# Last context chunk of each batch loaded on its own, into 80 partitions instead of 128

## The chip, the cores and the metric

The kernel runs on one core of one Trainium2 chip. The metric is the device time of the whole program in microseconds (us), the median over several runs. A profiled execution has a time of its own and a span, from the first to the last instruction, in which the trace shows every engine.

## What is computed

The reference is one layer of a perceiver-like network in float32, on x (32 batches x 64 rows x 512) and a context (32 batches x 1601 rows x 512). Three blocks follow each other: attention of x over the context, self-attention of x, and a mixture of eight experts with a shared expert. The change touches only the first block, for each batch:

```python
Sim = (enc @ w1)[:, :, None] + (ctx @ w2)[:, None, :] + einsum('bid,bjd->bij', enc * w3, ctx) + b_sim
A = softmax(Sim, axis=2)                 # 64 x 1601
hq_hat = einsum('bij,bjd->bid', A, ctx)  # 64 x 512
feats = concatenate([enc, hq_hat, enc * hq_hat, enc * hc_bar], -1)
hcq = feats @ W_qv + b_qv                # 2048 -> 512
```

`enc` is x after a layer norm, `ctx` the context. The context is thus used twice: once transposed (the scores) and once with its rows on the partitions (the weighted sum).

## The kernel before

**Tiles.** Two batches make one tile t of 128 rows (64 + 64), so there are T = 16 tiles. For each tile the context of both batches (h = 0, 1) is read from HBM twice: `ctxT[h]`, four pieces k of 128 partitions x 1601, and `ctxN[h]`, 128 partitions x 13 chunks x 512. A chunk c holds 128 context rows; 12 chunks are full (JM = 12) and the thirteenth has the last JT = 65 rows. In HBM the thirteenth chunk is padded to 128 rows, and each partition's 13 chunks lie side by side, so a partition's share of neighbouring chunks is one contiguous run.

**Loads.** All of this is issued by SyncE (SP). `load_ctx_T` (L437) loads a tile's `ctxT` in 8 transfers. `load_ctx_N` (L448) loads `ctxN` in four parts q (NP - 1 = 4), each once for either h: parts 0 to 2 have three chunks, the fourth has chunks 9 to 12. There is one buffer of each, so every load first waits for TensorE to have used that part of the tile before: `sim_done` counts the k of the scores, `pv_done` the groups of the weighted sum. Each transfer adds 16 to `ctxN_in[q]`, so TensorE waits for 32 per tile. The first tile is loaded at the start of the program, `ctxN` of it right after one piece of `ctxT`; then come rows of x and the weight `w_qv` (L459 to L461), then the loads for tile 1. Tiles 6 to 15 are loaded in a hardware loop of SP.

**TensorE.** The first tile's scores have a way of their own, so as not to wait for its `ctxT`: `first_T(q)` (L1896) transposes part q of `ctxN` by 36 instructions on TensorE in four parts, `first_T_end` (L1906) the last 65 rows, and `first_similar` (L1880) makes scores of them. From then on a tile goes through `stage_a`: transposes of small tiles (L1860, L1838), `features` (L1930 to L1947), `spread_max` (L1964), `exp_T` (L1970, 13 transposes of the softmax's numerators), `attend` (L1992, the weighted sum over 13 chunks, with `combined_chunk` L1955 between groups of three) and `similarities` (L1880, the next tile's scores). Tiles 2 to 13 are in a hardware loop with two tiles to a round. In `attend` TensorE waits for `ctxN_in[c // 3]` at c = 0, 3, 6, 9. The last chunk is read as `ctxN[h][0:65, 12, :]` only.

**After the first block** come weights for the other two blocks, loaded when `sim_done` has reached its last count, and then self-attention, router and experts. They use no context.

Of the kernel before, what the change touches and what calls it, by code (L numbers as in the profile page):

```python
# [29 lines left out]
JM = J // P  # L30
JT = J - JM * P
JC = JM + 1
JB = [(c * D, min(D, J - c * D)) for c in range(-(-J // D))]
NP = 5
H, HD = 16, 32
# [27 lines left out]
def perceiver_layer(nc, x, ctx_n, ctx_t, w1, w23, b_sim, w_qv, b_qv, wq, wk, wv, wm, b_qk, bv, bm,  # L63
# [8 lines left out]
    with ExitStack() as stack:  # L72
# [3 lines left out]
        def sem(name):  # L76
            return stack.enter_context(nc.semaphore(name))
# [42 lines left out]
        def within(name, lo, *dims, dt=F32):  # L120

            with nc.sbuf_tensor(name + "_lead", [P, lo], F32):
                with nc.sbuf_tensor(name, [P, *dims], dt) as v:
                    return v
# [5 lines left out]
        with nc.sbuf_tensor("raw_ws1", [P, KD, FS], F32) as raw_ws1:  # L130
# [3 lines left out]
        stage_at = [(ZERO_AT - 5 * KD * D, ZERO_AT - 4 * KD * D), (ZERO_AT - 3 * KD * D, ZERO_AT - 2 * KD * D),  # L134
                    (ZERO_AT - KD * D, ZERO_AT + D)]
        stage_raw = [within(f"stage_raw{i}", lo, KD, D) for i, (lo, _) in enumerate(stage_at)]
        zero = within("zero", ZERO_AT, D)
        wr_sb = within("wr_sb", stage_at[-1][1] + KD * D + D, KD, P)
# [4 lines left out]
        split_ws2 = within("split_ws2", WS, 2, KF, D, dt=F32R)  # L143
        W_QV = 2 * KD * J + 2 * JC * D
        HQ = W_QV + 6 * KD * D + J + -(W_QV + J) % 16 + JC * P + 2 * D
        w_mid = within("w_mid", W_QV + KD * D, 2 * KD, D)
# [8 lines left out]
        def carve(*dims):  # L155
            n = 1
            for d in dims:
                n *= d
            v = arena[:, used[0]:used[0] + n]
            used[0] += n  # L160
            if len(dims) == 2:
                v = v.rearrange("p (a b) -> p a b", b=dims[1])
            if len(dims) == 3:
                v = v.rearrange("p (a b c) -> p a b c", b=dims[1], c=dims[2])
            if len(dims) == 4:
                v = v.rearrange("p (a b c d) -> p a b c d", b=dims[1], c=dims[2], d=dims[3])
            return v

        def as_split(v, whole=split):
# [6 lines left out]
        ctxT = [carve(KD, J) for _ in range(2)]  # L176
        ctxN = [carve(JC, D) for _ in range(2)]
        w_qv_sb = carve(4 * KD, D)
# [4 lines left out]
        used[0] += -used[0] % 16  # L183
        ET = carve(JC, P)
        F2_hi, F2_lo, F3_hi = (split[:, lo:lo + KD * P].rearrange("p (k n) -> p k n", n=P)
                               for lo in range(used[0] - JC * P, used[0] - JC * P + 3 * KD * P, KD * P))
        hc = carve(D)
# [23 lines left out]
        Kbd = [carve(KD, 2, HR * S) for _ in range(2)]  # L211
        assert used[0] - 2 * KD * HR * S <= 2 * KD * J + 2 * JC * D, used[0]
        Vbd = [carve(2, H // 2, VW) for _ in range(2)]
# [87 lines left out]
        def bank(i):  # L301
            return ps[:, i, :]
# [45 lines left out]
        ctxN_in = [sem(f"ctxN_in{q}") for q in range(NP - 1)]  # L348
# [77 lines left out]
        def _(sp):  # L426
# [4 lines left out]
            def load_ctx_T(t, first, lo=0, hi=KD):  # L431
                for k in range(lo, hi):
                    if not first:
                        sp.wait_ge(sim_done, KD * t + (k + 1 - KD))
                    for h in range(2):
                        src = ctx_t[bass.ds(2 * t + h, 1), k].rearrange("o p n -> p (o n)")
                        sp.dma_start(ctxT[h][:, k, :], src).then_inc(ctxT_in[k], 16)  # L437

            def load_ctx_N(t, first):
                n = JM // (NP - 1)  # L440
                for q in range(NP - 1):
                    last = q == NP - 2
                    if not first:
                        sp.wait_ge(pv_done, NP * t if last else NP * t + (q + 1 - NP))
                    here = slice(n * q, JC if last else n * (q + 1))
                    for h in range(2):
                        one = ctx_n[bass.ds(2 * t + h, 1)].rearrange("o p c d -> (o p) c d")
                        sp.dma_start(ctxN[h][:, here, :], one[:, here, :]).then_inc(ctxN_in[q], 16)  # L448

            load_ctx_T(0, True, 0, 1)  # L450
            sp.dma_start(X[:, 1:2, :], x_v[:, 1:2, :]).then_inc(x_early, 16)
# [21 lines left out]
            with sp.Fori(TX - 1, T) as t:  # L473
                load_ctx_T(t, False)
                load_ctx_N(t, False)
# [590 lines left out]
        def _(dve):  # L1066
# [3 lines left out]
            def step(ins):  # L1070

                chain[0] += 1
                ins.then_inc(dve_step, 1)
                dve.wait_ge(dve_step, chain[0])
# [66 lines left out]
            def row_max(t, first):  # L1141
# [3 lines left out]
                if first:  # L1145
                    at_j, w = JB[-1]
                    step(v.reduce_max(rmax[:, 3:4], bank(3)[:, 0:w], AX))
# [132 lines left out]
            def block_maxima(n):  # L1280
                dve.wait_ge(first_scores, n + 1)
                step(v.reduce_max(rmax[:, n:n + 1], bank(n)[:, 0:JB[n][1]], AX))

# [549 lines left out]
        def _(pe):  # L1833
# [30 lines left out]
            def similarities(t, first):  # L1864
# [4 lines left out]
                for k in range(KD):  # L1869
                    pe.wait_ge(ctxT_in[k], 32 * (t + 1 if k == 0 else t))  # L1870
                    for n in range(len(JB)):
                        last = similar(n, k)
# [4 lines left out]
            def similar(n, k):  # L1877
                at_j, w = JB[n]
                for h in range(2):
                    last = mm(bank(n)[S * h:S * (h + 1), 0:w], qT[:, k, S * h:S * (h + 1)],  # L1880
                              ctxT[h][:, k, at_j:at_j + w], start=(k == 0), stop=(k == KD - 1))
                return last

            def first_T(q):

                n = JM // (NP - 1)
                pe.wait_ge(ctxN_in[q], 32)
                for k in range(1, KD):
                    for h in range(2):
                        g = 6 * q + 2 * (k - 1) + h  # L1890
                        if g == 0:
                            pe.wait_ge(F1_ready, 1)
                        if g >= 4:
                            pe.wait_ge((first_act, first_dve)[h], (g - 4) // 2 + 1)
                        for c in range(n):
                            last = nc.tensor.transpose(bank(4 + g % 4)[:, P * c:P * (c + 1)],  # L1896
                                                       ctxN[h][:, n * q + c, P * k:P * (k + 1)], ident[:, :])
                        last.then_inc(first_done, 1)
# [11 lines left out]
            def first_similar(n, pieces):  # L1910
# [3 lines left out]
                for k in range(1, KD):  # L1914
                    last = similar(n, k)
                    if n == len(JB) - 1:
                        last.then_inc(sim_done, 1)
                if n < len(JB) - 1:
                    last.then_inc(first_scores, 1)
# [29 lines left out]
            def combined_chunk(t, i, k):  # L1949
                if k == 0:  # L1950
                    pe.wait_ge(F1_ready, t + 1)
                pe.wait_ge(wc_ready, 2 * (KD * t + k + 1))
                for h in range(2):
                    r = slice(S * h, S * (h + 1))
                    last = mm(bank(5)[r, :], F1[i][:, k, r], Wc[:, h, :], start=False, stop=(k == KD - 1))  # L1955
                if k < KD - 1:
                    last.then_inc(wc_used, 1)
                else:
                    last.then_inc(feats_done, 1)
# [15 lines left out]
            def attend(t, i, first=False):  # L1975

                if not first:
                    pe.wait_ge(hq_ready, t)
                for c in range(JC):
                    w = P if c < JM else JT  # L1980
                    if c == 0:
                        pe.wait_ge(et_act, 2 * t + 1)
                    if c == 4:
                        pe.wait_ge(et_dve, 2 * t + 1)
                    if c == 8:
                        pe.wait_ge(et_act, 2 * t + 2)
                    if c == 12:
                        pe.wait_ge(et_dve, 2 * t + 2)
                    if c % 3 == 0 and c < JM:
                        pe.wait_ge(ctxN_in[c // 3], 32 * (t + 1))  # L1990
                    for h in range(2):
                        last = mm(bank(7)[S * h:S * (h + 1), :], ET[0:w, c, S * h:S * (h + 1)], ctxN[h][0:w, c, :],  # L1992
                                  start=(c == 0), stop=(c == JC - 1))
                    if c % 3 == 2 or c == JC - 1:
                        last.then_inc(pv_done, 1)
                    if c % 3 == 2 and not first:
                        combined_chunk(t - 1, 1 - i, c // 3)
# [410 lines left out]
            for u in range(TL):  # L2408
                for k in range(KF):
                    if u == 0:  # L2410
                        pe.wait_ge(lsh_ready, k + 1)
                    last = mm(last_bank[u], shT_l[:, k, P * u:P * (u + 1)], ws2_l[:, k, :],  # L2412
                              start=(k == 0), stop=(k == KF - 1))
# [57 lines left out]
```

## Time and profile before

| what | value |
|---|---|
| median of 3 runs | 1278.2 us (1277.79 to 1278.82) |
| the profiled execution | 1278.48 us |
| its span | 1276.8 us |
| TensorE (PE) busy in the span | 1251.5 us, 98% |
| mean clock granted to TensorE | 0.999 of full |
| read from HBM | 368.45 MB |

How to read it: 1.7 us of the profiled time lie outside of the span. TensorE's busy time holds what its pipelined matmuls overlap, so 98% says that it hardly ever stands still, not that it works at its peak. The context block takes the first 564 us or so, and there the DMA engines are busy too, with a share near 100%.

### The profile page before, as it was taken

What the parts mean: (1) busy time and instruction counts of PE and PEld (TensorE: products, weight loads), DVE (VectorE), ACT (ScalarE), POOL (GpSimd) and SP (SyncE); (2) the same over time, 40 slices, a digit from 0 to 9 for tenths busy, and PEclk for the clock granted to TensorE, in tenths of its full rate; (3) what the DMA queues carried; (4) which work ended last, traced back from release to release, by engine and by line L of the source; (5) the groups of instructions that cost most, each with busy time, mean ns of one, the idle gap of its engine ahead of it and who ended that gap; (6) DMA issues with size and microseconds to landing.
All of it is one profiled execution on the core that took longest, in us unless ns stands there. A gap on an engine that the chain in (4) does not pass through costs nothing.

```text
span 1276.8 us, 21920 instructions
## 1 busy us (share of the span) xinstructions
PE 1251.5 (98%) x7654; PEld 844.2 (66%) x7655; DVE 763.6 (60%) x1409; ACT 364.6 (29%) x593; POOL 173.8 (14%) x159
## 2 busy tenths in 40 slices
PE   5999999999999999999999999999999999999998
PEld 3344444444444444467888888899998888888843
DVE  4456555655454444478988877857543555555556
ACT  2322211212121211244555454542222233332300
POOL 1000000000000000003222223601430000000055
PEclk9999999999999999999999999999999999999999
DMA  9999999999999999833788778731749545554587
GB/s 353 411 418 416 415 415 419 419 419 418 419 419 416 392 396 390 316 134 123 253 285 276 256 266 305 281 132 59 275 170 333 169 155 188 186 185 158 170 324 247
DMA packets 103763, 375.95 MB, mean 294 GB/s; under 512 B 10656, under 2 KB 33184, under 8 KB 88992
## 3 DMA queue, kind: packets, MB, share of 16 engines
q1 hardware_dynamic: 98592, 358.52, 73.6%
q0 software_dynamic: 5120, 16.78, 3.7%
q8 instruction: 28, 0.46, 0.1%
q14 instruction: 23, 0.19, 0.0%
HBM read 368.45 MB, written 69.73 MB: 343 GB/s over the span
## 4 chain that ended last, share of the span: by engine, by line
PE 86%; DMA 7%; DVE 3%; issue 1%; ACT 1%; SPq 1%; POOL 0%; ACTq 0%; DVEq 0%; POOLq 0%
PE ps L1992 14%; PE ps L1880 13%; PE ps L2064 9%; PE ps L2054 9%; PE ps L2345 6%; PE ps L2348 6%; PE ps L2351 6%; DMA parts_low<-split 5%; PE ps L1955 4%; PE ps L1838 3%; PE ps L2412 2%; PE ps L2404 2%; PE ps L1970 2%; DMA arena<-ctx_n 2%; PE ps L1930 1%
## 5 line engine op out<-in xcount | busy, mean ns | idle before, releaser
L1992 PE MATMUL ps<-arena 128*64 128x512 f32 (+1 forms) x832 | 193.1, 596 | 0.0
L1880 PE MATMUL ps<-arena 128*64 128x512 f32 (+1 forms) x1024 | 177.6, 503 | 1.9 <-DVE arena L1138 1.2
L2064 PE MATMUL ps<-split 128*128 128x256 f32 x1344 | 170.6, 285 | 2.6 <-DVE split L1337 2.3
L2064 PEld LDWEIGHTS ps<-split 128*128 128x128 f32 x1344 | 163.7, 191 | 7.2 <-issue 4.7
L1880 PEld LDWEIGHTS ps<-arena 128*64 128x64 f32 x1024 | 65.0, 137 | 122.0 <-issue 119.4
L1992 PEld LDWEIGHTS ps<-arena 128*64 128x64 f32 (+1 forms) x832 | 58.4, 137 | 113.2 <-issue 112.6
L1234 DVE SCALAR_TENSOR_TENSOR arena<-arena,hbar 128x512 f32<-128x512 f32 x128 | 90.5, 749 | 67.9 <-PE ps L1955 66.3
L772 ACT ACTIVATE arena<-ps 128x512 f32<-128x512 f32 (+1 forms) x93 | 52.2, 581 | 241.9 <-PE ps L1955 180.2
L2054 PE MATMUL ps<-split 128*128 128x512 f32 x384 | 96.6, 400 | 1.1 <-DVE arena L1405 1.1
L1208 DVE TENSOR_TENSOR F<-arena,ps 128x512 f32<-128x512 f32 x16 | 11.0, 688 | 135.9 <-ACT split L817 135.9
L678 POOL TENSOR_TENSOR arena<-arena,row_b 128x512 f32 (+1 forms) x16 | 20.2, 1268 | 475.5 <-DVE arena L1108 448.1
L2054 PEld LDWEIGHTS ps<-split 128*128 128x128 f32 x384 | 69.7, 188 | 17.6 <-issue 2.0
L764 POOL DMA_INDIRECT arena<-moe_out,slot_i x32 | 34.0, 1063 | 271.4 <-DMA moe_out<-arena 262.0
L1955 PE MATMUL ps<-arena 128*64 128x512 f32 x256 | 66.0, 594 | 0.3 <-DVE arena L1234 0.3
L2054 PE MATMUL ps<-split_ws,split 128*128 128x512 f32 x264 | 61.1, 390 | 0.0
L817 ACT ACTIVATE split<-ps 128x256 fp32r<-128x256 f32 x32 | 10.5, 381 | 163.9 <-PE ps L1860 163.9
L2054 PEld LDWEIGHTS ps<-split_ws,split 128*128 128x128 f32 x264 | 49.2, 188 | 10.0
L772 ACT ACTIVATE arena<-arena 32x512 f32<-32x512 f32 x64 | 40.3, 630 | 34.0 <-DVE arena L1352 30.8
L1055 ACT ACTIVATE row_a<-ps 128x512 f32<-128x512 f32 x39 | 23.3, 598 | 82.1 <-PE ps L2351 82.1
L2345 PE MATMUL ps<-w_high,xT_p 128*128 x156 | 45.8, 415 | 0.2 <-issue 0.2
L753 POOL DMA_INDIRECT moe_in<-arena,idx x32 | 33.1, 1035 | 89.1 <-DVE idx L1736 81.7
L1838 PE MATMUL ps<-ident,arena 128*128 128x128 f32 x256 | 37.2, 276 | 8.0 <-DVE arena L1108 6.7
(229 smaller groups left out, 2007.5 us busy)
## 6 DMA issues: line engine op xcount, KB each, us to landing
arena<-ctx_t SPq DMA_DIRECT2D x122, 800.5 KB, 17.0
high<-parts_low SPq DMA_DIRECT2D x78, 1024.0 KB
arena<-ctx_n SPq DMA_DIRECT2D x96, 768.0 KB, 13.5
arena<-ctx_n SPq DMA_DIRECT2D x32, 1024.0 KB, 14.8
parts_high<-split SPq DMA_DIRECT2D x16, 1024.0 KB, 8.7
parts_low<-split SPq DMA_DIRECT2D x16, 1024.0 KB, 10.5
moe_in<-zero SPq DMA_DIRECT2D x3, 3328.0 KB, 17.5
moe_out<-arena SPq DMA_DIRECT2D x39, 256.0 KB, 2.1
```

Source lines behind the costliest of these rows:

```text
L764: nc.gpsimd.indirect_dma_start(y01[k][i], None, moe_out, bass.IndirectOffsetOnAxis(ap=slot_i[k][:, t:t + 1], axis=0)).then_inc(y01_in[i % ...
L772: return nc.scalar.activation(o, i, ACT.Copy)
L1234: v.scalar_tensor_tensor(Wc[:, h, :], w_qv_sb[:, 3 * KD + k, :], hbar[:, i, k, h:h + 1], w_qv_sb[:, k, :], ALU.mult, ALU.add).then_inc(wc_ ...
L1838: last = nc.tensor.transpose(dst[:, P * k:P * (k + 1)], src[:, P * k:P * (k + 1)], ident[:, :])
L1880: last = mm(bank(n)[S * h:S * (h + 1), 0:w], qT[:, k, S * h:S * (h + 1)], ctxT[h][:, k, at_j:at_j + w], start=(k == 0), stop=(k == KD - 1))
L1955: last = mm(bank(5)[r, :], F1[i][:, k, r], Wc[:, h, :], start=False, stop=(k == KD - 1))
L1992: last = mm(bank(7)[S * h:S * (h + 1), :], ET[0:w, c, S * h:S * (h + 1)], ctxN[h][0:w, c, :], start=(c == 0), stop=(c == JC - 1))
L2054: last = mm(dst, lhs[a][:, k, :], rhs[b][:, k, :], start=(k + i == 0), stop=(k == n - 1 and i == 2))
L2064: last = mm(dst[:, 2 * P * m:2 * P * (m + 1)], w[a][:, k, c], tokens[b][:, k, :], start=(k + i == 0), stop=(k == KD - 1 and i == 2))
L2345: mm(dst, parts[0][:, k, :], high_w(k), start=(k == 0), stop=False)
L2348: mm(dst, parts[1][:, k, :], high_w(k), start=False, stop=False)
L2351: last = mm(dst, parts[0][:, k, :], low_w(k), start=False, stop=(k == KD - 1))
```

## The change

The fourth load of `ctxN` takes chunks 9 to 11 only, and chunk 12 is loaded by a transfer of its own, into the first JP = 80 partitions (65 rounded up to a multiple of 16). Both count on `ctxN_in[3]`, so TensorE waits there for 64 per tile instead of 32. Nothing else is different; the padded rows 80 to 127 of the last chunk are no longer read from HBM.

```diff
@@ constants
 JC = JM + 1
+JP = -(-JT // 16) * 16
@@ load_ctx_N
-                    here = slice(n * q, JC if last else n * (q + 1))
+                    here = slice(n * q, n * (q + 1))
                     for h in range(2):
                         one = ctx_n[bass.ds(2 * t + h, 1)].rearrange("o p c d -> (o p) c d")
                         sp.dma_start(ctxN[h][:, here, :], one[:, here, :]).then_inc(ctxN_in[q], 16)
+                        if last:
+                            sp.dma_start(ctxN[h][0:JP, JM, :], one[0:JP, JM, :]).then_inc(ctxN_in[q], 16)
@@ first_T
-                pe.wait_ge(ctxN_in[q], 32)
+                pe.wait_ge(ctxN_in[q], 64 if q == NP - 2 else 32)
@@ attend
                     if c % 3 == 0 and c < JM:
-                        pe.wait_ge(ctxN_in[c // 3], 32 * (t + 1))
+                        pe.wait_ge(ctxN_in[c // 3], (64 if c // 3 == NP - 2 else 32) * (t + 1))
```

SP's program at the start, the first tile's `ctxN`, of before:

```order
L437 DMA arena<-ctx_t 128x1601 x2
L451 DMA arena<-x 128x512
L452 DMA bsim<-b_sim 128x1
L453 DMA row_a<-w 128x512
L448 DMA arena<-ctx_n 128x1536 x6
L448 DMA arena<-ctx_n 128x2048 x2
L455 DMA arena<-x 128x2x512
```

and of the change, where lines are 1 to 3 higher:

```order
L438 DMA arena<-ctx_t 128x1601 x2
L454 DMA arena<-x 128x512
L455 DMA bsim<-b_sim 128x1
L456 DMA row_a<-w 128x512
L449 DMA arena<-ctx_n 128x1536 x7
L451 DMA arena<-ctx_n 80x512
L449 DMA arena<-ctx_n 128x1536
L451 DMA arena<-ctx_n 80x512
L458 DMA arena<-x 128x2x512
```

The fourth part's two transfers of 128 x 2048 numbers have become four, 128 x 1536 and 80 x 512 for each h, at the same place; the same happens for every tile.

TensorE's program in the loop over tiles, `attend` of the round's first tile around chunk 9, of before:

```order
L1992 MATMUL ps<-arena 64x512 x4
L1986 REGISTER_ALU
L1992 MATMUL ps<-arena 64x512 x2
L1952 ISA
L1955 MATMUL ps<-arena 64x512 x2
L1992 MATMUL ps<-arena 64x512 x6
```

and of the change:

```order
L1995 MATMUL ps<-arena 64x512 x4
L1989 REGISTER_ALU
L1995 MATMUL ps<-arena 64x512 x2
L1955 ISA
L1958 MATMUL ps<-arena 64x512 x2
L1993 REGISTER_ALU
L1995 MATMUL ps<-arena 64x512 x6
```

One register instruction per tile is new, since 64 * (t + 1) is no longer the same number as 32 * (t + 1) of the other waits. No instruction of the other engines has moved.

## Rows read from the trace of the kernel before

**Rows 1.** The page: busy time by engine; slices of 1/40 of the span.
```profile
PE 1251.5 (98%) x7654; PEld 844.2 (66%) x7655; DVE 763.6 (60%) x1409; ACT 364.6 (29%) x593; POOL 173.8 (14%) x159
...
DMA  9999999999999999833788778731749545554587
```

**Rows 2.** Windows, three tiles' periods: us, busy us (instructions), PEclk, DMA share, GB/s.
```profile
71.48:105.36 33.88, 33.88 (x181) 15.87 (x180) 17.04 (x35) 5.36 (x12) 1.27 (x1) 1.00 1.02 416
...
376.70:410.63 33.93, 33.93 (x181) 15.86 (x180) 17.13 (x35) 5.37 (x12) 1.27 (x1) 1.00 1.02 416
410.63:444.51 33.88, 33.88 (x181) 15.87 (x180) 17.17 (x35) 6.64 (x13) 1.27 (x1) 1.00 0.99 394
```

**Rows 3.** Waits, 0 to 560 us: engine line <- releaser: total us, times, longest.
```profile
PE ps L1896 <- DMA arena<-ctx_n: 4.2, 3, 1.7
```

**Rows 4.** Waits of SP's own queue, 0 to 560 us.
```profile
SPq L448 <- PE ps L1992: 247.5, 58, 10.0
SPq L437 <- PE ps L1880: 83.3, 52, 2.8
```

**Rows 5.** DMA issues of the first 560 us: count, KB each, median us to landing.
```profile
arena<-ctx_t SPq DMA_DIRECT2D x122, 800.5 KB, 17.0
arena<-ctx_n SPq DMA_DIRECT2D x96, 768.0 KB, 13.5
arena<-ctx_n SPq DMA_DIRECT2D x32, 1024.0 KB, 14.8
...
w23c<-w SPq DMA_DIRECT2D x1, 4.0 KB, 2.4
```

**Rows 6.** Timeline of TensorE's first tile: start, us, instructions [idle before <-releaser].
```profile
24.71 2.18 PE L1896 MATMUL ps<-ident,arena 128*128 128x128 f32 x18
27.81 2.19 PE L1896 MATMUL ps<-ident,arena 128*128 128x128 f32 x18 [0.91 <-DMA arena<-ctx_n]
29.93 2.80 PE L1880 MATMUL ps<-arena 128*64 128x512 f32 x12
...
37.86 0.49 PE L1964 MATMUL ps<-arena,ones 128*128 128x128 f32 x2 [0.95 <-DVE arena L1160]
39.13 2.46 PE L1970 MATMUL ps<-ident,arena 128*128 128x128 f32 x13 [0.78 <-ACT arena L784]
```

**Rows 7.** The chain that ended last, 8 to 80 us: start, us, what.
```profile
8.10 19.67 DMA arena<-ctx_n
...
39.13 2.46 PE ps L1970 x13
41.59 12.12 PE ps L1992 x50
53.71 10.78 PE ps L1880 x47
...
71.48 1.42 PE ps L1970 x13
...
76.48 2.58 PE ps L1992 x12
```

**Rows 8.** Windows of the first tile, columns as in rows 2.
```profile
20.00:24.00 4.00, 3.26 (x22) 1.92 (x22) 1.65 (x3) 1.12 (x3) 0.00 (x0) 1.00 1.02 423
...
32.00:36.00 4.00, 4.00 (x30) 1.56 (x28) 1.05 (x2) 1.62 (x2) 0.54 (x1) 1.00 1.05 391
36.00:40.00 4.00, 2.27 (x25) 1.77 (x21) 2.68 (x10) 1.86 (x3) 0.00 (x0) 0.97 1.06 394
40.00:44.00 4.00, 4.00 (x16) 2.00 (x16) 3.03 (x9) 3.00 (x7) 0.00 (x0) 0.60 1.03 420
```

**Rows 9.** Loads of `ctx_t` issued from 38 to 39 us, the last for tile 1.
```profile
L437 SPq DMA_DIRECT2D arena<-ctx_t x2: 430/430/431, 37.9 to 38.4; - x2
...
DMA to landing us min/median/max: 17.2/18.2/19.2
```

**Rows 10.** All instructions on `ctx_n`: duration ns min/median/max, first and last start.
```profile
L448 SPq DMA_DIRECT2D arena<-ctx_n x128: 327/333/5614, 4.4 to 529.2; - x128
```

## The prediction

> **What bounds the kernel now.** I read the page first. It shows two things near their limit in the context block: TensorE, busy 98% of the whole span, and the DMA engines, whose slices read 9 up to about 45% of it [rows 1]. A change that takes bytes away is worth something only if the second of them ends a wait of the first, so the next view is the windows, one for each tile's period. From 71 us on there are 13 such periods of close to 33.9 us (three shown) and TensorE is busy through all of each [rows 2]. Busy can hide a slower pace, so I checked the pace in the chain: 12 matmul passes of the weighted sum take 2.58 us [rows 7], 0.215 us for each pass of 512 columns, and the same stands in every period.
>
> The best test lies in the DMA column of the same windows. Up to 410 us the engines move 416 to 419 GB/s (416 in both windows shown), after that 394, and the period is the same 33.88 to 33.93 us [rows 2]. A tile needs 8 x 800.5 + 6 x 768 + 2 x 1024 = 13,060 KB = 13.37 MB [rows 5], which at 418 GB/s is 32.0 us, and 13.37 MB in 33.9 us is 394 GB/s: the rate that the later window shows. So the DMA engines first work off a backlog (x and weights come on top), and then they only follow TensorE. The waits say it too. Over 560 us TensorE waits for a context load only in the first tile's transposes, three times and 4.2 us in all [rows 3], while SP's queue waits 247.5 us for the weighted sum and 83.3 us for the scores to give buffers back [rows 4]. The chain passes through a DMA transfer once in this block: the one issued at 8.10 us, which lands 19.67 us later [rows 7]. That is the last half of the first tile's fourth part, the very one that is changed.
>
> **The change, part by part.**
>
> *Bytes of each tile.* The fourth part was 2 x 1024 KB. It becomes 2 x (768 + 80 x 2 KB) = 2 x 928 KB, so 192 KB or 0.197 MB less for a tile, 3.1 MB for 16. At 418 GB/s that would be 0.47 us of DMA time for a tile and 7.5 us for all, were the DMA engines the limit. They are not: from tile 1 on the saving only makes 32.0 us into about 31.6 us under TensorE's 33.9 us. Worth 0. The cover is TensorE's own work. Without it (a TensorE period under 32 us) the 7.5 us would be real.
>
> *The first tile.* Here TensorE waits. It ends the third part's transposes at 24.71 + 2.18 = 26.89 us and starts the fourth's at 27.81 us, idle for 0.91 us, released by the DMA [rows 6]. The fourth part's 2.097 MB at the 423 GB/s of that time [rows 8] take 4.96 us. What replaces them: 1.573 MB in three-chunk rows at 423 GB/s, 3.72 us, and 0.328 MB in rows of 2 KB. The trace has no such rows of `ctx_n`, but `w_qv` has the same 2 KB rows and is what runs from 32 to 36 us, at 391 GB/s [rows 8]: 0.84 us. Sum 4.56 us, so the part lands 0.40 us earlier. Bounds: at 423 GB/s throughout the gain is 0.46 us; the upper end of any gain here is the whole idle time, 0.91 us. On the other side, if the added transfers brought a cost of their own of 0.2 us each (two of them), nothing is left; and if each brought the 2.4 us that even a 4 KB transfer takes from issue to landing [rows 5], 4.8 us are added. I take 0.40 us, since seven transfers of this queue stood behind each other there and the engines still moved 423 GB/s, so that a transfer's own latency lies beside its neighbours' data.
>
> *Does the 0.40 us reach the end?* Behind the fourth part's transposes TensorE goes on without a wait for DMA; its next idle times, 0.95 and 0.78 us, are released by VectorE and ScalarE [rows 6], which themselves follow the scores, so they move along. The loads for tile 1 must still be in time: the last `ctx_t` is issued at 38.4 us and lands 19.2 us later at the most, at 57.6 us [rows 9], and TensorE comes to that piece three quarters into the scores that start at 53.71 us and take 10.78 us [rows 7], at 61.8 us. There are 4.2 us to spare, and the load too has less in front of it. Behind that everything is the same chain, 0.40 us earlier.
>
> *SP.* Two more issues per tile, at 0.33 us each, the median of the 128 that are there [rows 10]. The half h = 1 of the fourth part is issued that much later. SP waits 330 us in this block [rows 4], and loads land 13.5 to 17 us after their issue [rows 5] for a use half a period away. At the start SP issues the eight loads far ahead of the data. 0.
>
> *TensorE's register instruction*, one for each of 12 tiles in the loop. TensorE's sequencer already has such instructions at the same kind of place, ahead of chunk 8, and periods in the loop (33.88 and 33.93 us in turn) are those of tile 1 outside of the loop, 33.88 us [rows 2]. The 0.05 us of the slower ones is all that a round's branch and its register instructions cost, so the upper bound is 12 x 0.05 = 0.6 us; below, 0. I take 0, because the queue of matmuls ahead covers it. *Waits at 64 instead of 32*: a different number, no cost.
>
> *Sum*: -0.40 us against the profiled 1278.48 us, 1278.1 us. The median of the three runs is 1278.2 us, 0.3 us under the profiled one, so the forecast of the median is 1277.8 us. The three runs lie 1.0 us apart, so this cannot be told from nothing; about 0.2% (2.6 us) is what a measurement of this kernel can tell from no change.
>
> **A rule against the change.** The trace first: three-chunk transfers of 768 KB, each with a completion of its own, run at 423 GB/s back to back [rows 8]. The Trainium skill, DMA: Bandwidth & Descriptors, section on measured bandwidth, fits 2.0 us plus bytes at 436 GB/s for one DMA and asks for 1 MiB or more in each. Read as a cost on the queue, it would give 786 KB in 3.8 us, 207 GB/s; the trace has twice that, so the fixed part must be latency which later transfers hide. With it as a queue cost the first tile would get 4.0 us longer for the two added transfers, less the 0.45 us of bytes.
>
> **The rivals.**
>
> *A fixed cost on the DMA engines for each added transfer (slower).* Place: the fourth part, 2 for each tile. After the change a tile's loads take 31.6 us of a 33.9 us period; the slack is 2.3 us, so this decides only where an added transfer costs more than about 1.15 us of all engines. At the 2.4 us of the smallest transfer [rows 5] the period becomes 31.6 + 4.8 = 36.4 us, 2.5 us over, times 15 tiles = 37 us, and 4.4 us at the start: 1278.2 + 41 = 1320 us. For it: only that no small transfer stands in the middle of this stream. Against it: 423 GB/s above. 2 in 100. By the Trainium skill's 2.0 us (DMA: Bandwidth & Descriptors, measured bandwidth), read as a cost on the queue, the period would be 35.6 us and the time near 1307 us.
>
> *The 80 partitions are spread over few engines (slower).* All context loads of before have 128 partitions, so nothing in the trace shows what 80 do. 0.328 MB over n engines at 26.1 GB/s each (418 / 16) add 12.5 / n us to those engines' 12.85 MB / 418 GB/s = 30.7 us; that passes 33.9 us where n is under 4. With n = 1 the period is 43.3 us and the time 1278 + 15 x 9.4 = 1419 us; with 5 or more nothing is lost but some 1.2 us at the start. The Trainium skill, same page, section on why a DMA counts by 16, says that the largest divisor up to 16 of the partition count sets the engines, which gives 16 for 80; no run here shows it yet. 2 in 100.
>
> *The clock (either way).* Behind the two idle times after the scores the granted clock falls: 0.97 in the mean from 36 to 40 us and 0.60 from 40 to 44 us [rows 8], that is, part of it at 1.2 instead of 2.4 GHz. Its price by rows at both levels: the 13 transposes take 2.46 us there and 1.42 us a tile later, and the first tile's 52 passes of the weighted sum 12.12 us instead of 52 x 0.215 = 11.2 us [rows 7], 2.0 us in all. The idle time moves forward by 0.4 us; if that makes the fall go away, the time is 1278.2 - 2.0 - 0.4 = 1275.8 us. 4 in 100. If instead a second fall is added in the first tile, it costs about as much: 1278.2 - 0.4 + 2.0 = 1279.8 us. 3 in 100. The idle time in front of the scores only shrinks, so I have no reason for either.
>
> *Nothing at all.* If the transposes of the fourth part were held by something else directly behind the DMA, such as VectorE's copies, 0 is won: 1278.2 us. 9 in 100.
>
> **How the numbers follow.** The forecast has the remaining 80 in 100. Its own range is the bounds of the sum, -0.91 to +0.6 us, and half of the runs' scatter, 0.5 us: 1276.8 to 1279.3 us. Slower by over 0.2% are the two cost rivals, 4 in 100. Faster by over 0.2% (under 1275.6 us) needs the fall to vanish and a little more: 3 in 100. Same: 93 in 100. The range takes in the clock's going away, 1275.8 us, and ends at 1279.3 us.
>
> **What would show it.** The timeline of the changed kernel should have the fourth part's transposes start near 27.4 us with 0.5 us of idle time before them, periods of 33.9 us as before, the later windows at 13.18 MB / 33.9 us = 389 GB/s, and HBM reads lower by 3.1 MB, at 365.3 MB. Wrong would be: a wait of TensorE on `ctx_n` or `ctx_t` behind the first tile, periods over 34.1 us, a fourth part that lands later than 27.8 us, or a granted clock that falls at another place.

## The result

The change made the kernel slower: 1285.0 us in the median of 6 runs (1282.6 to 1286.7) against 1278.0 us (6 runs of before), a ratio of 1.0048 with a 95% interval of 1.0036 to 1.006, which is some 6 us. The forecast was 1277.8 us and no change that can be measured.

The profiled execution took 1282.6 us, the quickest of the six. Its page:

```profile
span 1280.9 us, 22004 instructions
...
PE 1252.9 (98%) x7654; PEld 845.0 (66%) x7655; DVE 763.8 (60%) x1409; ACT 364.7 (28%) x593; POOL 173.1 (14%) x159
...
DMA  9999999999999999962787778731648545554587
...
HBM read 365.30 MB, written 69.73 MB: 340 GB/s over the span
```

HBM reads fell by the 3.15 MB that were forecast. TensorE is busy 1.4 us longer (1251.5 before, [rows 1]) in a span that is 4.1 us longer. In the DMA row the 9s reach one slice further than before: fewer bytes take longer.

The first tile in TensorE's timeline (start, us, instructions, idle before and releaser) answers to [rows 6]:

```profile
24.59 2.19 PE L1899 MATMUL ps<-ident,arena 128*128 128x128 f32 x18
28.96 2.19 PE L1899 MATMUL ps<-ident,arena 128*128 128x128 f32 x18 [2.18 <-DMA arena<-ctx_n]
31.08 2.80 PE L1883 MATMUL ps<-arena 128*64 128x512 f32 x12
...
40.28 2.33 PE L1973 MATMUL ps<-ident,arena 128*128 128x128 f32 x13 [0.78 <-ACT arena L787]
```

The fourth part's transposes wait 2.18 us for their load, where it was 0.91 us; they start at 28.96 instead of 27.81 us, 1.15 us later, where 0.40 us earlier was forecast. (The experiments below put the growth of this wait between 0.5 and 1.3 us.) The waits of TensorE for loads over the first 600 us:

```profile
PE ps L1899 <- DMA arena<-ctx_n: 4.8, 3, 2.2
...
PE ps L1883 <- DMA arena<-ctx_t: 3.9, 5, 1.1
```

The second row is new in the steady part, the tiles behind the first: four of its five waits, 2.8 us, lie behind 70 us. Before there was none. Nearly all of it falls into one tile's period, first of the change and then of before:

```profile
208.70:245.49 36.79, 34.16 (x178) 15.78 (x177) 21.09 (x49) 8.14 (x15) 1.27 (x1) 1.00 1.02 392
```

```profile
207.21:241.09 33.88, 33.88 (x181) 15.87 (x180) 21.47 (x49) 8.14 (x15) 1.27 (x1) 1.00 1.02 418
```

It follows the loads of x for tiles 7 to 15, which SP issues at 140 and 177 us in the change and which land 21 to 24 us later. Longer windows show how the DMA engines fared (columns as in [rows 2]; the last three are granted clock, DMA share and GB/s). The change:

```profile
70.00:240.00 170.00, 167.38 (x885) 77.23 (x884) 92.41 (x198) 31.72 (x65) 6.33 (x5) 1.00 1.02 392
240.00:380.00 140.00, 139.81 (x735) 66.83 (x734) 72.52 (x144) 25.59 (x52) 5.06 (x4) 1.00 1.02 394
380.00:480.00 100.00, 100.00 (x531) 46.25 (x530) 49.80 (x98) 16.41 (x37) 3.80 (x3) 1.00 1.02 393
480.00:545.00 65.00, 64.67 (x343) 28.96 (x342) 32.06 (x72) 11.44 (x25) 1.27 (x1) 1.00 1.02 394
```

and the kernel before in the same stretches:

```profile
70.00:240.00 170.00, 170.00 (x898) 79.56 (x897) 95.61 (x201) 32.64 (x67) 6.33 (x5) 1.00 1.02 417
240.00:380.00 140.00, 140.00 (x745) 66.37 (x745) 72.77 (x150) 26.14 (x58) 5.07 (x4) 1.00 1.02 418
380.00:480.00 100.00, 100.00 (x531) 47.02 (x529) 49.74 (x96) 16.41 (x33) 3.80 (x3) 1.00 1.00 402
480.00:545.00 65.00, 64.65 (x336) 28.82 (x333) 31.91 (x70) 12.30 (x25) 1.27 (x1) 1.00 0.91 354
```

Saturated DMA engines (share 1.02, the highest of these long windows) moved 417 GB/s before and move 392 GB/s now. From about 410 us on the earlier kernel had worked off its backlog [rows 2]; in the changed one the share stays at 1.02 up to 545 us. The loss is not spread evenly. In windows of 2 us inside one tile's period of the change the rate collapses when the fourth part is in the queues, and is whole otherwise:

```profile
382.00:384.00 2.00, 2.00 (x15) 1.15 (x15) 1.93 (x8) 1.76 (x6) 0.00 (x0) 1.00 1.04 303
384.00:386.00 2.00, 2.00 (x12) 0.68 (x10) 1.97 (x6) 0.03 (x1) 0.00 (x0) 1.00 1.01 334
386.00:388.00 2.00, 2.00 (x12) 0.62 (x10) 1.62 (x4) 0.00 (x0) 0.00 (x0) 1.00 1.02 400
...
398.00:400.00 2.00, 2.00 (x12) 0.63 (x10) 1.77 (x4) 0.00 (x0) 0.00 (x0) 1.00 1.02 418
...
412.00:414.00 2.00, 2.00 (x10) 1.64 (x9) 1.93 (x6) 1.01 (x1) 0.00 (x0) 1.00 1.02 332
414.00:416.00 2.00, 2.00 (x15) 1.77 (x14) 1.89 (x5) 0.70 (x3) 0.00 (x0) 1.00 1.02 303
```

The share stays at 1.0: the engines do not idle in the dip, their transfers just take longer, all of them and not only the small one. The trace's records of single DMA packets show it. From 382 to 386 us a packet of `ctx_t` (6404 bytes) took 320 ns in the mean, one of the three-chunk rows (6144 bytes) 328 ns and one of 2048 bytes 110 ns. In split128 below, which keeps the full rate, the means for these sizes from 70 to 240 us are 248, 239 and 87 ns.

### The profile page after: what moved, and what is told of

Same layout as the page of the kernel before. It is cut to its first block, busy times and chain, and to the rows that moved or that the text cites. A ratio compares the mean times of both kernels' runs of the same rounds, so it can differ in the third digit from the quotient of the medians.

```text
span 1280.9 us, 22004 instructions
## 1 busy us (share of the span) xinstructions
PE 1252.9 (98%) x7654; PEld 845.0 (66%) x7655; DVE 763.8 (60%) x1409; ACT 364.7 (28%) x593; POOL 173.1 (14%) x159
## 2 busy tenths in 40 slices
DMA packets 106835, 372.81 MB, mean 291 GB/s; under 512 B 11168, under 2 KB 33696, under 8 KB 96160
## 4 chain that ended last, share of the span: by engine, by line
PE 79%; DMA 11%; SPq 4%; DVE 3%; issue 2%; ACT 1%; POOL 0%; ACTq 0%; DVEq 0%; POOLq 0%
PE ps L1995 12%; PE ps L1883 10%; PE ps L2067 9%; PE ps L2057 9%; PE ps L2348 6%; PE ps L2351 6%; PE ps L2354 6%; DMA parts_low<-split 5%; DMA arena<-ctx_t 4%; PE ps L1958 4%; PE ps L1841 3%; PE ps L2415 2%; PE ps L2407 2%; SPq L438 2%; PE ps L1973 2%
```

## The experiments

**How they are read.** The chips of the experiments scatter more than the first: before itself ran from 1275.7 to 1296.5 us there. Most of the scatter lies behind the context block: from the last tile's L1970 transposes to the end of the span the profiles of all kernels here take 730 to 742 us, 730.7 us in before and 734.9 us in split128, whose context block is that of before. So each profile is read in two numbers of the context block beside the ratio: TensorE's idle time ahead of the fourth part's transposes in the first tile, and the time from the 13 transposes of the softmax (L1970 in before) of tile 1 to those of tile 15, 14 periods. In before that is 71.32 to 546.12 us, 474.80 us; with the change 72.46 to 550.90 us, 478.44 us, 3.6 us more. The idle time is the better sign in the first tile, since what goes before shifts the start itself by a microsecond: in later_only, whose first tile is that of before, the same transposes start at 28.85 us behind 0.90 us of idle time. There is one profile of each kernel. Where a diff below leaves lines out, "..." marks the place.

Theory A: an 80-partition transfer over 16 DMA engines gives the engines rows of other partitions than a 128-partition load does, and this out-of-place writing slows all loads around it. (The pages bear out the 16: packets under 512 B rise from 10656 to 11168 by the change, 16 for each of the 32 added transfers.) Theory B: rows of 2 KB, or two more transfers per tile, are slow by themselves.

**split128**, the padded chunk as a transfer of its own:

```diff
-JP = -(-JT // 16) * 16
+JP = P
```

> The change with the last chunk's own transfer over all 128 partitions (the padded rows too), so the bytes are those of before. Theory A (placement): 80 partitions over 16 DMA engines give each engine rows that in a 128-partition load belong to another engine, both slow each other down, and the slowdown goes away here. Then DMA moves 414 to 418 GB/s in the context block, the first tile's fourth transposes start at 27.7 to 28.0 us, and the time is that of before, 1277.5 to 1279.0 us. Theory B (rows of 2 KB and two more transfers per tile are slow by themselves): rate near 392 GB/s as with the change, 1284 to 1286 us.

Ratio 0.9972 (0.9933 to 1.001), 474.8 us for the 14 periods, no wait for a load behind the first tile, idle time 1.06 us. The times expected for theory A were missed (a start at 28.52 us, a median of 1282.3 us), but before beside it ran at 1283.4 us in the median, and what counts, rate and periods, came out as theory A says. Windows:

```profile
70.00:240.00 170.00, 170.00 (x898) 79.60 (x897) 95.62 (x203) 32.63 (x67) 6.32 (x5) 1.00 1.02 415
240.00:380.00 140.00, 140.00 (x744) 66.64 (x744) 72.80 (x148) 26.82 (x58) 5.08 (x4) 1.00 1.02 417
```

The same number of transfers and as many rows of 2 KB and more, at 415 GB/s: theory B falls. This pair shows what costs the time, since split128 and the change differ in `JP` alone, 128 against 80. With more bytes than the change it is as fast as before.

**rows80**, the change's bytes in long rows:

```diff
-                        sp.dma_start(ctxN[h][:, here, :], one[:, here, :]).then_inc(ctxN_in[q], 16)
                         if last:
-                            sp.dma_start(ctxN[h][0:JP, JM, :], one[0:JP, JM, :]).then_inc(ctxN_in[q], 16)
+                            four = slice(n * q, JC)
+                            sp.dma_start(ctxN[h][0:JP, four, :], one[0:JP, four, :]).then_inc(ctxN_in[q], 16)
+                            sp.dma_start(ctxN[h][JP:P, here, :], one[JP:P, here, :]).then_inc(ctxN_in[q], 16)
+                        else:
+                            sp.dma_start(ctxN[h][:, here, :], one[:, here, :]).then_inc(ctxN_in[q], 16)
```

> The change's bytes with no rows of 2 KB: the fourth part is loaded as partitions 0 to 79 with four chunks (8 KB rows) and partitions 80 to 127 with three (6 KB rows), two transfers for each h, as many as with the change. Theory A (placement): now the whole fourth part is out of place, 1.9 MB a tile instead of 0.33 MB, so it is slower than the change, 1290 to 1330 us. Theory B (2 KB rows): as fast as before, 1277 to 1279 us; if the number of transfers costs, 1284 to 1286 us.

Ratio 1.0822 (1.0733 to 1.0911), 1391.4 us, worse than either theory's range for it. 579.84 us for the 14 periods (78.56 to 658.40), 41.4 us for each. The waits of TensorE behind 60 us and a window:

```profile
PE ps L1998 <- DMA arena<-ctx_n: 40.6, 18, 4.5
PE ps L1886 <- DMA arena<-ctx_t: 33.6, 26, 4.5
```

```profile
70.00:240.00 170.00, 157.94 (x807) 74.19 (x803) 86.77 (x179) 30.25 (x63) 5.06 (x4) 0.98 1.02 343
```

There are no 2 KB rows of context, and it is the worst but one of all: with 1.9 MB a tile in transfers of fewer than 128 partitions instead of 0.33 MB, the rate is 343 instead of 392 GB/s. The waits in the 14 periods are 74 of the 105 us that they are longer; the granted clock over them is 0.96 in the mean where before had 1.00, so part of the rest is TensorE at a lower clock.

**halves**, the kernel before with the fourth part cut at partition 64, as many bytes and the same rows of 8 KB:

```diff
-                        sp.dma_start(ctxN[h][:, here, :], one[:, here, :]).then_inc(ctxN_in[q], 16)
                         if last:
-                            sp.dma_start(ctxN[h][0:JP, JM, :], one[0:JP, JM, :]).then_inc(ctxN_in[q], 16)
+                            four = slice(n * q, JC)
+                            for r in (slice(0, S), slice(S, P)):
+                                sp.dma_start(ctxN[h][r, four, :], one[r, four, :]).then_inc(ctxN_in[q], 16)
+                        else:
+                            sp.dma_start(ctxN[h][:, here, :], one[:, here, :]).then_inc(ctxN_in[q], 16)
```

> The kernel before with only its fourth part's transfer cut into partitions 0 to 63 and 64 to 127, four chunks each: same bytes, same 8 KB rows, two more transfers per tile. Theory A (placement): 16 engines write into half of the partitions at a time, the fourth part of 2.1 MB runs at about half of 420 GB/s, 5 us more a tile, and a period becomes about 37 us in place of 33.9: 1300 to 1330 us. Theory B: rows are long, so at most the cost of the added transfers, 1278 to 1286 us.

Ratio 1.0944 (1.0843 to 1.1044), 589.78 us for the 14 periods (80.39 to 670.17), 42.1 us each where I expected 37. TensorE waits 83 us for loads in them; the other 32 us of the 115 us are not waits for loads, and here too the granted clock is lower, 0.95 in the mean. So more than a quarter of the loss is not the DMA engines' directly. The idle time in the first tile:

```profile
25.54 2.18 PE L1902 MATMUL ps<-ident,arena 128*128 128x128 f32 x18 [0.37 <-DMA arena<-ctx_n]
35.74 4.10 PE L1902 MATMUL ps<-ident,arena 128*128 128x128 f32 x18 [8.01 <-DMA arena<-ctx_n]
```

This is the strongest case. Source rows, their length and the bytes are those of before, and the two more transfers cost nothing in split128. What differs is that a transfer reaches 64 partitions, and with that, presumably, which engine reads and writes which rows. The packet records show that the loss is in the packets and not between them: from 70 to 240 us a packet of 8192 bytes takes 588 ns in the mean, where it took 315 ns in before. The Trainium skill, SBUF — State Buffer, section "Door 1: The DMA port swizzle", says that partitions 0 to 63 reach only 8 of SBUF's 16 DMA ports. The run agrees in direction, with packets that take 1.87 times as long. The neighbouring 128-partition loads suffer too: the 6144-byte packets take 260 instead of 238 ns in the mean of that stretch, and 390 to 600 ns in each microsecond from 113 to 118 us, while the halves are moved.

**split96** and **p112**, the change with `JP = 96` and `JP = 112`:

> The change with 96 partitions instead of 80 for the last chunk (6 rows for each of 16 engines). Theory A (placement): still out of place, 1283 to 1290 us, with a DMA rate of 385 to 400 GB/s. Theory B: as the change, 1284 to 1286 us. It tells the two apart little, but says whether 80 is a special count.

> The change with 112 partitions for the last chunk, 7 rows for each of 16 engines. Theory A: nearly all rows are still out of place, DMA 380 to 400 GB/s, 482 to 492 us from the second tile's transposes to the last's (96 partitions: 484.9). If the loss were only from partitions left idle (128 - 80), it shrinks to a third: 408 GB/s or more and 474.8 us.

Ratios 1.008 (1.0044 to 1.0117) and 1.0159 (1.0103 to 1.0214); 484.9 and 485.64 us for the 14 periods; split96's median of 1294.8 us lies above the range expected for it. The windows of split96 and then of p112:

```profile
70.00:240.00 170.00, 164.42 (x861) 74.14 (x862) 90.29 (x191) 29.38 (x61) 6.33 (x5) 1.00 1.02 388
```

```profile
70.00:240.00 170.00, 165.50 (x867) 75.68 (x867) 92.23 (x197) 31.05 (x63) 6.32 (x5) 1.00 1.02 388
```

80 is no special count, and idle partitions are not the loss: with 16 of them instead of 48 it is no smaller. Of all the counts tried, only 128 in one transfer has the full rate.

**own80**, the source of the 80 rows contiguous, in a tensor of its own:

```diff
-                            sp.dma_start(ctxN[h][0:JP, JM, :], one[0:JP, JM, :]).then_inc(ctxN_in[q], 16)
+                            sp.dma_start(ctxN[h][0:JP, JM, :], ctx_r[bass.ds(2 * t + h, 1)].rearrange("o p d -> (o p) d")).then_inc(ctxN_in[q], 16)
```

> The change with the last chunk's 80 rows taken from a tensor of their own, where they lie contiguous (160 KB), instead of 2 KB pieces 26 KB apart. If the reading side is what is slow, the rate goes back to 410 GB/s or more and the 474.8 us of before come back. Theory A (the writing side: rows out of place among the engines): no difference, 385 to 396 GB/s.

Ratio 1.0044 (1.0025 to 1.0064), 479.21 us, and the rate is that of the change:

```profile
70.00:240.00 170.00, 166.99 (x882) 76.84 (x881) 91.95 (x194) 30.73 (x64) 6.34 (x5) 1.00 1.02 394
```

So the gaps between the 2 KB pieces on the reading side are not the cause. (The main tensor's partitions are one chunk shorter here as well, which changed the rate no more.)

**placed** and **unplaced**, 65 rows in three transfers:

```diff
-                            sp.dma_start(ctxN[h][0:JP, JM, :], one[0:JP, JM, :]).then_inc(ctxN_in[q], 16)
+                            for lo in (0, 32):
+                                sp.dma_start(ctxN[h][lo:lo + 32, JM, :],
+                                             one[lo:lo + 32, JM, :].rearrange("(a b) d -> a b d", b=4)
+                                             ).then_inc(ctxN_in[q], 16)
+                            sp.dma_start(ctxN[h][64:65, JM, :], one[64:65, JM, :]).then_inc(ctxN_in[q], 16)
...
```

(unplaced without the `rearrange`; TensorE's two waits become 128 per tile in both).

> The last chunk's 65 rows in three transfers for each h: rows 0 to 31 and 32 to 63, each with the source written as 8 groups of 4 rows, which should put it on 8 DMA engines with 4 rows each, the rows that the same engines have in a 128-partition load; then row 64 alone. Fewer bytes than before the change, more transfers (8 in the fourth part instead of 4 with the change). Theory A (placement): rows are with their own engines, so the slowdown goes: the last tile's transposes of the softmax start at 546 to 547.5 us (546.28 before, 551.06 with the change), DMA near 410 GB/s while there is a backlog. Theory B (small rows and many transfers): worse than the change, 555 us or later, total 1288 us or more.

> The same three transfers of the same rows as in the run named placed, but the source is not written in groups, so each 32-row transfer goes over 16 engines with 2 rows each. Theory A (placement): engines 2 to 15 write rows of others, so the slowdown is there again: last tile's transposes at 550 to 556 us, DMA 385 to 400 GB/s. Theory B: the same as placed, since rows and transfers are the same.

Ratios 1.0036 (1.0007 to 1.0065) and 1.0028 (1.0013 to 1.0044); both 393 to 394 GB/s from 70 to 240 us, 474.9 and 474.8 us for the 14 periods, both 2.67 us idle in the first tile. This pair failed as a test: both show the same count of packets under 512 B on the page, 11712, so the grouping of the source did not put the transfers on fewer engines, and the two are one kernel in that respect. Neither could theory A's own prediction for placed, a rate near 410 GB/s, be tried in this way. What they do show is that the lowered rate alone need not make TensorE wait behind the first tile. Their tile needs 13.12 MB instead of the change's 13.18 MB (128 + 2 KB for each h instead of 160 KB), and the waits in the steady part are gone; that the 0.06 MB are the reason is argued from the slack worked out below, and other small differences of the transfers are not ruled out.

**first_only** and **later_only**, the change for tile 0 alone and for tiles 1 to 15 alone (there `own = last and not first`):

```diff
-                    here = slice(n * q, n * (q + 1))
+                    own = last and first
+                    here = slice(n * q, JC if last and not own else n * (q + 1))
...
-                        if last:
+                        if own:
...
```

> The change for the first tile alone, all other tiles load the fourth part as before. The fourth transposes of the first tile start at about 29.0 us as with the change (27.81 before), and nothing else waits: last tile's transposes at 547.4 us, total about 1.1 us over before. If the disturbance stays in the queues behind the first tile, it is later than that.

> The change for all tiles but the first. The fourth transposes of the first tile start at 27.8 us as before; from tile 1 on the DMA engines move 392 instead of 418 GB/s, the extra loads of x at tiles 4 and 5 are not worked off, and TensorE waits for ctx_t or ctx_n between 200 and 320 us by 3 to 4 us in all: last tile's transposes at 549.3 to 550.5 us.

first_only: idle time 1.59 us in the first tile and 474.8 us behind it, 417 GB/s from 70 to 240 us; the disturbance does not outlast its tile. Its median is all the same 4 us above before's, of which its profile, the quickest of the five executions, shows less than 1 us. later_only: idle time 0.90 us, then 482.4 us for the 14 periods at 389 GB/s, and more waits than in the change: the 14 periods are 7.6 us longer than in before, where I had 3 to 4. Ratios 1.0033 (1.0015 to 1.0051) and 1.0045 (1.0026 to 1.0064). The loss has two places, as supposed; their sizes vary from run to run. With the small transfers in the first tile the idle time there is 2.18, 2.00, 1.68 (own80) and 1.59 us (first_only); without them it is 0.91, 0.90 and 1.06 us (split128).

**again**, the change itself on another chip.

> The change once more, on another chip, beside before. From the second tile's transposes of the softmax to the last tile's: 474.8 us in before and 478.4 in the first profile of the change. I expect 477 to 483 us here, all of the surplus in waits for ctx_t or ctx_n, and a ratio of 1.003 to 1.006.

Ratio 1.0035 (1.0018 to 1.0053), 477.72 us for the 14 periods, 2.00 us idle in the first tile; ratio and periods lie in the ranges expected.

**x_filled**, without the two loads of x tiles 7 to 15:

```diff
-                if t == TX - 3:
-                    sp.dma_start(X[:, TX:TY, :], x_v[:, TX:TY, :]).then_inc(x_in[0], 16)
-                if t == TX - 2:
-                    sp.dma_start(X[:, TY:T, :], x_v[:, TY:T, :]).then_inc(x_in[1], 16)
...
+            nc.gpsimd.memset(X[:, TX:TY, :], 1.0).then_inc(x_in[1], 16)
+            nc.gpsimd.memset(X[:, TY:T, :], 1.0).then_inc(x_in[1], 16)
...
```

> The change, with the two loads of x tiles 7 to 15 (2.36 MB) left out; GpSimd fills those tiles with 1.0 at the start, so the output is another one. If the stalls come because the DMA engines at 392 GB/s are just as fast as the loads need (389) and what comes on top is no longer worked off, they go away without these loads: no wait of TensorE for a load between tiles 1 and 15, 474.8 us from the second tile's transposes to the last's, with the DMA rate in the backlog still at 385 to 396 GB/s. If the stalls are short collisions that do not depend on a backlog, they stay, 477 us or more.

474.86 us (72.92 to 547.78), no wait for a load behind the first tile, at a rate as low as ever:

```profile
70.00:240.00 170.00, 170.00 (x899) 79.57 (x898) 95.60 (x203) 32.41 (x66) 6.33 (x5) 1.00 1.02 391
240.00:380.00 140.00, 140.00 (x744) 67.08 (x744) 72.75 (x148) 26.70 (x54) 5.07 (x4) 1.00 1.02 386
```

The low rate alone costs the steady part nothing here; in the change it costs behind the loads of x, in the period of 36.79 us above. Its total, ratio 1.0018 (0.9997 to 1.004), also holds another routing of the experts, since x is another, and is not compared.

| kernel | GB/s, 70 to 240 us | idle, first tile, us | 14 periods, us |
|---|---|---|---|
| before | 417 | 0.91 | 474.8 |
| split128 | 415 | 1.06 | 474.8 |
| first_only | 417 | 1.59 | 474.8 |
| the change | 392 | 2.18 | 478.4 |
| again | 394 | 2.00 | 477.7 |
| own80 | 394 | 1.68 | 479.2 |
| later_only | 389 | 0.90 | 482.4 |
| split96 | 388 | 1.66 | 484.9 |
| p112 | 388 | 2.29 | 485.6 |
| placed, unplaced | 393, 394 | 2.67, 2.67 | 474.9, 474.8 |
| x_filled | 391 | 2.13 | 474.9 |
| rows80 | 343 | 5.43 | 579.8 |
| halves | 344 | 8.01 | 589.8 |

## Why the prediction was wrong, step by step

**What bounds the kernel.** Right for before: no wait for a load behind the first tile, periods set by TensorE, and the first tile's fourth part the one load on the path.

**"Bytes of each tile ... worth 0."** This step failed first. The bytes were right (3.15 MB less), but I turned them into time at the old 418 GB/s, as though what a transfer costs were its bytes over the rate of the stream. Measured, a tile's 13.18 MB at 392 GB/s take 33.6 us, not the 31.6 us of the forecast (31.5 us by its own numbers) and more than the 32.0 us of before. Against 31.5 us at full rate that is 2.1 us, or 1.05 us for each added transfer. The first rival named a price of this size and set its point at 1.15 us, then called it 2 in 100. Its mechanism was not right either: split128 adds as many transfers and pays nothing. The price is that of a transfer which reaches fewer than 128 partitions, and all loads beside it pay.

**That point was wrong too.** It weighed a tile's loads against a tile's period and left out what comes on top. In 33.9 us the engines moved 418 x 33.9 = 14.17 MB before, 0.80 MB more than a tile needs; by that the 2.36 MB of x tiles 7 to 15 are worth three tiles. At 392 GB/s they move 13.29 MB, 0.11 MB more than the tile needs, and three tiles become about twenty, more than there are. Both are estimates from these rates; what the traces show is a share of 1.02 up to about 410 us before and up to 545 us now. My own first view had this backlog in it [rows 2]. x_filled shows it (no x, no waits); placed and unplaced fit it (0.06 MB a tile less, no waits).

**The first tile.** I priced the 80 rows by `w_qv`'s 2 KB rows at 391 GB/s, 0.84 us, and got 0.40 us of gain. The nearest row by length was the wrong neighbour: `w_qv` has all 128 partitions. split128 says that 2 KB rows in place cost little (idle time 1.06 us against 0.91). The term was to be -0.40 us and came out as a wait 1.27 us longer, since the collapse also hit the large transfers beside the small ones. The window from 22 to 30 us moves

```profile
22.00:30.00 8.00, 5.82 (x39) 3.74 (x39) 2.33 (x5) 1.93 (x4) 0.00 (x0) 1.00 1.03 321
```

321 GB/s with the change, and 389 GB/s before:

```profile
22.00:30.00 8.00, 7.09 (x50) 4.84 (x52) 3.39 (x6) 2.76 (x6) 0.00 (x0) 1.00 1.01 389
```

**"The 80 partitions are spread over few engines."** The rival that looked at the right thing asked the wrong question of it, how many engines instead of which partitions each of them writes. I let the count of 16 settle it, and 16 engines there were, by the small packets of the pages.

**"Does the 0.40 us reach the end?"** The carrying along was right in this pair: the first tile's 1.15 us is there in full at tile 1 (72.46 against 71.32 us). In own80 it is not, by a fall of the granted clock that stayed away (last section).

**SP, the register instruction, the waits at 64.** Worth nothing, as forecast: in split128 they are all there and the 14 periods take 474.8 us.

**The check that misled.** The forecast said that late windows would show 389 GB/s as a sign that DMA merely follows TensorE. The windows of the change show 393 and 394 GB/s there, and it is the engines' limit; before showed 394 GB/s where it was not [rows 2]. The figure alone cannot tell the two apart. The share can, if barely: 0.99 with 394 GB/s before [rows 2], 1.02 with 393 GB/s from 380 to 480 us now. It is plainer where before's loads run out, from 480 to 545 us: 0.91 before, 1.02 now.

**The sum.** In the profile: 1.15 us in the first tile, 3.64 us in the steady part, together 4.8 us of the context block, and 0.7 us less behind it, for 4.1 us of span. The 0.7 us are within what that part scatters. The surplus of the 14 periods varies (2.9 to 7.6 us in the two profiles of the change and that of later_only), and the profiled execution was the quickest of its six. The median's 6 us may be a larger dose of the same, but this is not shown: none of the slower executions is profiled, and the medians of first_only, placed and unplaced lie some 4 us above before's with no loss in their steady part.

**What stays open.** Which engine writes which partitions of an 80-partition transfer is not in the trace. That a transfer which reaches fewer than 128 partitions slows the loads around it is shown by split128 against the change, and by halves. That the reason lies on the writing side is what own80 leaves, since another source layout changed nothing; but the number of partitions may also set which engine reads which rows, and no run parts the two. That two engines meet at one SBUF port is only argued: the 588 ns of halves for a packet that took 315 ns fit it, and the pair that should have moved rows to their own engines did not move them. Nor was a version found that beats before: behind the first tile TensorE waited for no load there, so there was nothing to win.

## What to carry to other kernels

Where loads of 128 partitions saturate the DMA engines, do not price a load of fewer partitions by its bytes alone. Here two of 160 KB in each tile took the whole stream from 417 to 392 GB/s, and padding to all 128 was the cheaper choice. Before calling a slack of 2 us per tile cover, divide what comes on top (a backlog, one-off loads) by the surplus that is left after the change. And price an operation by a row that shares its shape over the partitions, not only its row length.

## What the runs showed that was not expected

The loss does not shrink with the number of partitions left out (388 GB/s with 96 and with 112 against 392 with 80), and with 128 partitions cut into 64 and 64 a period took 24% longer with not one byte changed.

The fall of the granted clock in the first tile goes away in some executions. In own80 the window from 40 to 44 us has a full clock where before had 0.60 [rows 8]:

```profile
40.00:44.00 4.00, 4.00 (x27) 2.12 (x27) 3.05 (x9) 3.25 (x7) 0.00 (x0) 1.00 1.04 419
```

From the fourth part's transposes to tile 1's are then 41.88 us (28.47 to 70.35) instead of 43.51 us (27.81 to 71.32). The fall costs 1.6 us, not the 2.0 us that the prediction worked out; the same 41.9 us stand in split96 and later_only. With the fall there are 43.5 us in before, the change and most others, whether it comes at 40 us or, as in p112, at 30 to 34 us (0.61 and 0.53 of full). In unplaced, where a second one follows the first, the stretch is 45.2 us. The prediction had named both, the fall going away and a second one, as rivals.
